# Mixed spectra loaded five steps ahead, results stored in 256 KB pieces from 128 partitions

## What is computed

```
h = einsum('bhwi,ic->bhwc', x, fc0_w) + fc0_b          # 32 images, 64 channels
for l in range(4):
    xf = rfft2(h)                                       # 32 x 16 modes are kept
    top, bot = einsum('bixy,ioxy->boxy', xf[modes], w1[l] / w2[l])
    sc = irfft2(top and bot put back, zeros elsewhere)
    y  = sc + einsum('bihw,oi->bohw', h, pw_w[l]) + pw_b[l]
    h  = gelu(batchnorm(y) * gamma[l] + beta[l])
h = gelu(h @ fc1_w + fc1_b) @ fc2_w + fc2_b             # then attention and experts
```

## Time and profile before

| | |
|---|---|
| median of 3 runs | 3170.56 us (3169.16 to 3171.28) |
| profiled execution | 3177.74 us |
| its span, first to last instruction | 3175.6 us |
| PE busy, share of the span | 2511.6 us, 79% |
| ACT, DVE busy | 1567.9 us (49%), 1576.0 us (50%) |
| DMA, mean busy share of 16 engines (queue of SP) | 64.7% |
| mean granted TensorE clock | 0.886 |

### The profile page before, as it was taken

The page is one execution under the profiler, slowest core; times in us unless marked ns, Lnnn a source line. Parts: engine busy times, 40 slices in busy tenths (PEclk is TensorE's granted clock), DMA queues, the critical chain, the costliest instruction groups (busy, mean ns, idle before and its releaser), DMA issues. The chain is left out here.

```text
span 3175.6 us, 75376 instructions
## 1 busy us (share of the span) xinstructions
PE 2511.6 (79%) x32251; PEld 1645.9 (52%) x32251; DVE 1576.0 (50%) x2552; ACT 1567.9 (49%) x2659; POOL 191.7 (6%) x237
## 2 busy tenths in 40 slices
PE   6668879967777799667778987777879757784899
PEld 4655546656454466655455657544522246652344
DVE  3146667722455677235556752455510186655343
ACT  1213347722454676234456752344579747761333
POOL 0000000000000000000000000000000033220443
PEclk9779989988888899878888998888889979996999
DMA  8947789866888997778889967788875300001442
GB/s 247 245 118 181 187 246 324 289 150 185 243 253 243 299 317 237 178 201 247 240 243 305 323 206 179 216 242 242 249 229 178 94 1 1 1 1 25 97 92 62
DMA packets 243690, 604.34 MB, mean 190 GB/s; under 512 B 28415, under 2 KB 108991, under 8 KB 241087
## 3 DMA queue, kind: packets, MB, share of 16 engines
q1 hardware_dynamic: 243359, 599.51, 64.7%
HBM read 396.12 MB, written 203.93 MB: 189 GB/s over the span
## 5 line engine op out<-in xcount | busy, mean ns | idle before, releaser
L618 ACT ACTIVATE work<-P,small 128x512 f32<-128x512 f32 x512 | 323.7, 683 | 617.4 <-PE P L491 614.5
L384 PE MATMUL P<-cst,work 128*128 128x128 f32 (+1 forms) x3760 | 549.2, 286 | 56.1 <-ACT work L636 21.8
L384 PEld LDWEIGHTS P<-cst,work 128*128 128x128 f32 (+1 forms) x3760 | 412.2, 144 | 213.6 <-issue 166.6
L472 PE MATMUL P<-cst,work 64*64 64x64 f32 x8192 | 192.9, 260 | 261.0 <-DMA work<-G_d 252.6
L491 PEld LDWEIGHTS P<-cst,ATs 64*128 64x128 f32 x4096 | 267.7, 200 | 241.0 <-issue 132.9
L439 PE MATMUL P<-W,work 128*64 128x64 f32 x4096 | 282.3, 307 | 131.5 <-ACT work L589 131.1
L753 DVE COPY work<-P 128x512 f32<-128x512 f32 x256 | 175.0, 686 | 360.4 <-PE P L472 360.4
L439 PEld LDWEIGHTS P<-W,work 128*64 128x64 f32 x4096 | 280.7, 238 | 134.0 <-issue 97.1
L760 DVE BATCH_NORM_STATS2 W<-work 128x6 f32<-128x512 f32 x512 | 326.9, 680 | 9.7 <-ACT work L618 9.5
L472 PEld LDWEIGHTS P<-cst,work 64*64 64x64 f32 x8192 | 172.5, 170 | 287.0 <-DMA work<-G_d 224.1
L491 PE MATMUL P<-cst,ATs 64*128 64x128 f32 x4096 | 318.0, 298 | 0.0
(11 more groups left out here) (166 smaller groups left out, 2864.6 us busy)
## 6 DMA issues: line engine op xcount, KB each, us to landing
work<-z_d SPq DMA_DIRECT2D x384, 512.0 KB, 6.1
z_d<-work SPq DMA_DIRECT2D x256, 512.0 KB, 6.1
W<-in_wmix SPq DMA_DIRECT2D x96, 512.0 KB, 6.7
X_d<-work SPq DMA_DIRECT2D x128, 256.0 KB, 5.0
work<-X_d SPq DMA_DIRECT2D x32, 1024.0 KB, 12.5
G_d<-work SPq DMA_DIRECT2D x128, 256.0 KB, 3.3
work<-G_d SPq DMA_DIRECT2D x256, 128.0 KB, 5.0
hz<-z_d SPq DMA_DIRECT2D x64, 512.0 KB, 4.6
```

Source lines behind the costliest of these rows:

```text
L384: return nc.tensor.matmul(out, in_, ident[0:n, 0:n], start=True, stop=True, is_transpose=True)
L472: last = nc.tensor.matmul(P[v][g * 64:g * 64 + 64, m * 64:m * 64 + 64], Gt[a.par][o, x:x + 64], i1c[o, k:k + 64], start=True, stop=True)
L618: nc.scalar.activation(ychunk(a, h), P[4 + 2 * (a.q % 2) + h][:, :], ACT.Identity, bias=bias0 if first else pwb_c).then_inc(S["eY"], 1)
```

## The change

In the code, `load_mixed` is the four loads of L301. It is called for pair 0 before the first step and then, at q = 0 of a pair, for the next pair (`At(t, u, q, -4)`). A store now takes one result of 128 partitions, 256 KB, at every step, two in a step. Its DRAM side is, for one image h and quarter k, the runs of n = 512 pixels (2 KB) of all g and o, g outermost. The number of stores is doubled, so the counts on `yst` are too.

```
-        z_y = z_d.rearrange("(t u) (h o) (g k n) -> t u g k o h n", u=2, h=2, g=2, k=2)
+        z_y = z_d.rearrange("(t u) (h o) (g k n) -> t u h k g o n", u=2, h=2, g=2, k=4)
...
+                def load_mixed(n):
+                    for v in range(2):
+                        for h in range(2):
+                            sp.dma_start(Gt[n.par][v * 64:v * 64 + 64, h * 512:h * 512 + 512], G_s[h, n.t, n.par, v]).then_inc(gl[n.par], 16)
+                load_mixed(At(0, 0, 0, 0))
+
                 def step(t, u, q):
                     a = At(t, u, q, 0)
-                    if q == 0 and a.ok:
-                        wait(sp, "pI1", l * 32 + a.pair * 2 - 2)
-                        for v in range(2):
-                            for h in range(2):
-                                sp.dma_start(Gt[u][v * 64:v * 64 + 64, h * 512:h * 512 + 512], G_s[h, a.t, u, v]).then_inc(gl[u], 16)
+                    n = At(t, u, q, -4)
+                    if q == 0 and n.ok:
+                        wait(sp, "pI1", l * 32 + n.pair * 2 - 2)
+                        load_mixed(n)
                     b = At(t, u, q, 8)
-                    if b.ok and b.q % 2 == 1:
+                    if b.ok:
 
                         sp.wait_ge(S["eY"], l * 128 + b.s * 2 + 2)
-                        for g in range(2):
-                            sp.dma_start(z_y[b.t, b.par, g, b.q // 2], ybuf[b.q // 2][g * 64:g * 64 + 64, :].rearrange("p (h n) -> p h n", h=2)).then_inc(yst[b.q // 2], 16)
+                        for h in range(2):
+                            sp.dma_start(z_y[b.t, b.par, h, b.q], ychunk(b, h)).then_inc(yst[b.q // 2], 16)
...
-                    sp.wait_ge(yst[u], (l + 1) * 16 * 32)
+                    sp.wait_ge(yst[u], (l + 1) * 16 * 64)
...
-                                    act.wait_ge(yst[a.q // 2], (l * 16 + a.pair) * 32)
+                                    act.wait_ge(yst[a.q // 2], (l * 16 + a.pair) * 64)
```

## The result

The changed kernel takes 5004.31 us (median of 4 runs, 5002.81 to 5008.16), the kernel before in the same rounds 3170.92 us. The ratio is 1.577, with a 95% interval of 1.574 to 1.581. The forecast was 5160 us in a range of 4990 to 5470.

The account below looks back on a forecast made before the run. The order on SP was taken to bound the inverse stages; two-engine stores would make them 811 us (27 + 688 + 91 + 5), 756 in layer 0: 1990 us more, 3177.7 + 1990 = 5168, less 7, 5160 us; range 4990 to 5470.

Parts of the forecast that it names:

- What bounds the kernel before: Inverse stages: the order on SP sets the pace, 19.75 us a pair; PE has 7 us to spare, the queue 3.6.
- the ring: Inverse-stage pair: L472's results let SP store, only then SP issues the four L301 loads that the next L472 awaits; 4.53 us idle.
- The stores on two engines: New inverse-stage stores, 2x64x512: all carried by the same 2 of 16 DMA engines, 64 packets of 2 KB on each.
- The price of a 2 KB packet: Stores on one DMA engine: 84 ns a packet, between 80 and 89; 688 us of stores per layer.
- The share of the loads on these engines: Loads on each of the two store engines: 91 us a stage, 36 us in layer 0.
- Head and close: Inverse stage: 27 us from its start to the first store, 5 us from the last store's issue to the next stage.
- The loads ahead at nothing: Mixed-spectra loads one pair earlier: up to 4.5 us a pair by itself, costed at nothing because another queue is later.
- PE's 203 us a stage: Inverse stage: PE needs 203 us, 12.7 us a pair, and stays hidden.
- Rival A: Inverse-stage stores use all 16 engines, or different pairs at once, so the kernel is faster: 2900 to 2950 us; 8%.
- Rival B: Inverse-stage stores run on two engines that also idle between stores, 635 us more: 5800 us; 10%.
- The signs to look for: Inverse stages: DMA share about 25%, 95 to 105 GB/s, pair some 48 us, L312 issues 5 us each without landing time.

Follow-up runs that it names:

- the sweep over 2, 4, 8 and 16: Changed kernel with its stores' DRAM side at 2 (other row order), 4, 8 or 16 outermost: 5006.9, 3722.6, 3117.3, 2892.1 us; values not the reference's.
- 128x512: Changed kernel with each store's DRAM side as one row for each of 128 partitions (values not the reference's): 2888.9 us, ratio 0.907 to the kernel before.
- 16x8x512: Changed kernel with the same stores but 16 outermost on the DRAM side (values not the reference's): 2892.1 us, ratio 0.910 to the kernel before.
- 64x2x512: Changed kernel with each step's 512 KB stored as two 64-partition transfers in 2 KB runs, to the right places: 2939.6 us, ratio 0.924 to the kernel before.

## Why the prediction was right, and where it was off

*What bounds the kernel before: right.* The order on SP set the pace. With the loads taken out of the ring alone, 202 us went.

*The stores on two engines: right, and it is nearly everything.* Three arrivals for each store, no landing time, and the sweep over 2, 4, 8 and 16. That the two are always the same was read from four-row stores. It is borne out by the stretch of stores alone: stores in a row on different pairs of engines would have overlapped, but only two packets start in every 80 ns, and each store takes 5.12 us.

*The price of a 2 KB packet: mis-sized.* I took 84 ns, halfway between the 80 ns that the 4 KB stretch gave and the 89 ns on the line to 512 B packets. 5.12 us for 64 packets are 80 ns. A layer's stores then take 128 x 5.12 = 655 us instead of 688, four times 33 = 132 us of what the forecast was too high. The line through 512 B packets was the wrong one to lean on. A pair adds up to 8 x 5.12 + 5.1 + 1.3 = 47.4 us, measured 47.3.

*The share of the loads on these engines: right.* It is the 6.4 us of that sum. Layer 0, which has fewer of them, is 768.6 - 715.9 = 53 us shorter in a stage, forecast 811 - 756 = 55 us.

*Head and close: somewhat too large.* In layer 1 the first store is issued 1248.59 - 1225.89 = 22.7 us after the stage's start, where I took 27, and the rest lasts 745.9 us where 655 + 91 + 5 make 751. The stores and loads of that sum, 746 us, are right. The close is too large: the last store's packets end at 1994.05 us in the trace, 0.5 us before the next stage. (SP's last issue, from which I had counted the close, is no measure of it here: in layer 3 it ends at 4088.43 + 40.96 = 4129.39 us, 13.8 us before the next stage, because stores still stand in the queues.) Over the four stages this is 35 us (3189 - 132 = 3057 forecast, 3022 measured). Against the profiled execution of 5003.3 us the forecast of 5168 is 165 us too high: 132 of packets and 35 of this, with 2 us the other way outside the stages. The 7 us that I took off for the median were not there this time.

*The loads ahead at nothing: right in this kernel.* They give about 8 us, by a single execution without them. In the three kernels whose stores run on all 16 engines they are worth 121 to 202 us.

*PE's 203 us a stage: too low, without effect.* The three steps of the earlier trace rows that it was read from leave out the step right behind the wait, whose L472 took 1.98 us at 1483.71 us; the next, at 1492.73 us, took 1.16. PE was busy 234 us in the stage of layer 1 before, at a granted clock of 0.84, and 275 us after, at 0.64; the 208.5 us of the 128x512 stage, at 0.97, are close to my figure. It stayed hidden in 768.6 us as forecast.

*Rival A* lost, but its price was nearly good: I gave 2900 to 2950 us if all engines carry a store, and 128x512 takes 2888.9 us, 16x8x512 2892.1. *Rival B* lost too. The two engines do not stand idle between stores: 64 packets started 80 ns apart fill the 5.12 us of a store.

The Trainium skill, "DMA: Bandwidth & Descriptors", section "Why a DMA increments its semaphore by 16 and not by 1", has the rule that one transfer runs on the largest number of engines up to 16 that divides the slowest dimension of both sides. The runs agree for 2, 4, 8 and 16, by their arrivals and their times, with the same source of 128 partitions throughout. The Trainium skill, "SBUF — State Buffer", section "Door 1: The DMA port swizzle", has as a sister rule that 64 partitions reach half the ports. The runs agree in direction: with the loads ahead, 128x512 beats 64x2x512 by 51 us. The two also write other rows, so the ports are not shown to be the cause.

*The signs to look for.* The share of the DMA engines is 30.0% (forecast 25), the rate 100 GB/s (forecast 95 to 105). The pair lasts 47.3 us (forecast 48). SP's issues do not take 5 us for each L312 while loads stand among them: two take 4.10 to 6.03 us, and as much of the holding up falls on L322, which stands behind them.

## What to carry to other kernels

Look at the outermost dimension of both sides of a transfer before you look at its partitions and the length of its runs: 2 there left 14 of the 16 DMA engines out of the stores, and the kernel took 5004 us; the same bytes in the same number of stores with 16 there took 2892 us, 9% less than the kernel before (ratio 0.910). A group of transfers without a landing time in the list of issues is the sign to look for. And a wait that a profile names is worth what the next limit leaves of it: the same early loads gave about 8 us beside stores on two engines, and 121, 125 and 202 us beside three forms of stores on 16.

## What the runs showed that I had not expected

PE's busy time for the same instructions is no constant: the matmuls of the stage of layer 2 took 214.0 us with the loads ahead alone and 239.1 in the kernel before, at granted clocks of 0.95 and 0.84.

With all engines at work the queue moves 336 GB/s through a stage of mixed loads and stores (128x512), and 64-partition stores cost less than the 15.4 GB/s an engine of the earlier trace rows suggest. With the loads ahead, stores from 64 partitions in runs of 2 KB still let 323 GB/s through the stage of layer 2, 20 GB/s an engine. Smaller stores at every step beat longer ones at every other step by 37 us, with a DMA share of 0.97 or more in both. What makes the difference stays open.
